# Causal attention of a fused transformer block: reordered casts, sums and transposes, and w(w+2) computed on GpSimd in two instructions

## The reference

```python
tq = jnp.sqrt(1.0 / curv + jnp.sum(q * q, axis=-1, keepdims=True))
tk = jnp.sqrt(1.0 / curv + jnp.sum(k * k, axis=-1, keepdims=True))
inner = jnp.einsum('bhtd,bhsd->bhts', q, k) - tq * jnp.swapaxes(tk, -1, -2)
arg = jnp.maximum(-curv * inner, 1.0 + 1e-07)
dis = jnp.sqrt(1.0 / curv) * jnp.arccosh(arg)
scores = 1.0 / (eps + dis) + _causal_bias(q.shape[-2], k.shape[-2], q.dtype)
return jnp.einsum('bhts,bhsd->bhtd', jax.nn.softmax(scores, axis=-1), v)
```

## Time and profile before

| | |
|---|---|
| three runs | 4958.24, 4977.92, 4982.76 us, median 4977.92 |
| profiled execution | 4974.08 us, of it the span 4972.4 us |
| busy, share of the span | PE 78%, PEld 50%, DVE 69%, ACT 42%, POOL 12% |
| mean granted TensorE clock | 0.88 of full speed |

### The profile page before, as it was taken

How to read it: one execution, slowest core, us unless ns; L and a number is a source line. 1 busy time by engine, 2 the same in 40 slices (tenths; PEclk the granted TensorE clock), 3 DMA queues, 4 the chain that set the end, 5 groups by cost and what they waited for, 6 DMA issues and landing times. The chain is left out here.

```text
span 4972.4 us, 89619 instructions
## 1 busy us (share of the span) xinstructions
PE 3898.1 (78%) x25263; PEld 2472.9 (50%) x25263; DVE 3431.8 (69%) x7462; ACT 2095.3 (42%) x3970; POOL 581.7 (12%) x1014
## 2 busy tenths in 40 slices
PE   6999799800048988857777776888799999799998
PEld 5777588600025555535555554666444444455554
DVE  4555444388967887867777775667677777477777
ACT  1222144476533333336767675233366666011110
POOL 0111100000000000010000000222111111122221
PEclk8999999955569989968888887899799999899999
DMA  2222144488954444444444443777555544211110
GB/s 80 75 73 77 56 172 175 171 242 276 400 213 128 125 129 122 123 89 91 94 94 92 94 93 71 177 194 195 133 123 123 123 121 100 75 51 51 57 54 29
DMA packets 508033, 616.80 MB, mean 124 GB/s; under 512 B 62202, under 2 KB 428509, under 8 KB 507933
## 3 DMA queue, kind: packets, MB, share of 16 engines
q1 hardware_dynamic: 498684, 614.41, 44.3%
q0 software_dynamic: 9248, 1.18, 0.2%
HBM read 345.06 MB, written 269.21 MB: 124 GB/s over the span
## 5 line engine op out<-in xcount | busy, mean ns | idle before, releaser
L1231 PE MATMUL ps<-k_downT,f_o 128*91 128x256 f32 x1152 | 261.2, 386 | 455.2 <-DVE f_o L1139 455.1
L3158 PE MATMUL ps<-m_we,m_xT 128*128 128x512 f32 x1104 | 507.4, 604 | 0.0
L2489 DVE TENSOR_REDUCE e_neg<-ps 128x2 f32<-128x546 f32 x512 | 369.7, 723 | 121.2 <-PE ps L2264 112.1
L1231 PEld LDWEIGHTS ps<-k_downT,f_o 128*91 128x91 f32 x1152 | 183.6, 162 | 524.4 <-issue 456.2
L2426 ACT ACTIVATE e_probT<-ps 128x546 f32<-128x546 f32 x512 | 320.6, 627 | 231.4 <-PE ps L2270 226.8
L3093 DVE SCALAR_TENSOR_TENSOR m_acc<-ps,m_weight,m_acc 128x256 f32<-128x256 f32 x552 | 257.6, 480 | 119.2 <-PE ps L3158 105.4
L3158 PEld LDWEIGHTS ps<-m_we,m_xT 128*128 128x128 f32 x1104 | 203.5, 192 | 212.7 <-issue 195.6
L587 DVE TENSOR_REDUCE b_new<-b_gu 128x1 f32<-128x1638 f32 x64 | 119.0, 1859 | 211.5 <-ACT b_gu L654 211.5
L2264 PE MATMUL ps<-e_k,e_q 96*128 96x273 bf16 x1024 | 213.1, 292 | 28.3 <-POOL e_block_mask L2222 16.1
L654 ACT COPY b_gu<-ps 128x273 f32<-128x273 f32 x384 | 148.5, 387 | 189.0 <-PE ps L692 189.0
L2270 PE MATMUL ps<-e_q,e_k 99*128 99x273 bf16 x1024 | 208.3, 285 | 9.3 <-DMA e_q<-e_shift 1.4
(11 more groups left out here) (375 smaller groups left out, 9040.7 us busy)
## 6 DMA issues: line engine op xcount, KB each, us to landing
s_gate<-b_gu SPq DMA_DIRECT2D x32, 819.0 KB, 4.0
s_up<-b_gu SPq DMA_DIRECT2D x32, 819.0 KB, 3.7
c_g<-s_gate SPq DMA_DIRECT2D x32, 819.0 KB, 7.0
s_gated<-c_g SPq DMA_DIRECT2D x32, 819.0 KB, 8.4
d_g<-s_gated SPq DMA_DIRECT2D x32, 819.0 KB, 10.7
d_u<-s_up SPq DMA_DIRECT2D x32, 819.0 KB, 10.6
s_o<-d_o SPq DMA_DIRECT2D x32, 819.0 KB
f_o<-s_o SPq DMA_DIRECT2D x32, 819.0 KB, 4.6
```

Source lines behind the costliest of these rows:

```text
L1231: last = nc.tensor.matmul(ps[0:R, t // 2, (t % 2) * D:(t % 2 + 1) * D], o[:, u, k, t * R:(t + 1) * R], downT[:, k, :], start=(k == 0), sto ...
L2489: nc.vector.tensor_reduce(neg[:, u, g // 2, :, 4 * (g % 2) + a], ps[:, bank:bank + 2, 0:T], AX.X, ALU.max, negate=True).then_inc(S["looked ...
L3158: last = nc.tensor.matmul(ps[0:R, EBANK[m % 4], :], xT[:, u, k, t * R:(t + 1) * R], we[:, k, 2 * p:2 * p + 2, :].rearrange("p e d -> p (e ...
```

## The change

The product w(w+2) leaves DVE. GpSimd computes it in two instructions, hu = w + 2 and hu = hu * w, with a semaphore `hu2` between them; it waits for the clamp and for the earlier batch's `add_root`, which reads `hu`. Further, PE emits MAIN 3 and PRE 6 to 8 ahead of `turn` 1; ACT does exponential 3 ahead of `first_part_hyp` and exponential 4 ahead of `second_part_hyp`, and `second_part` ahead of two of the `log_of_distance`; DVE does `top_scores` ahead of `remainder_hyp`, `largest` 0 ahead of `third_part_hyp`, and `add_shift` 3 ahead of `third_part`.

```diff
@@ block.gpsimd
-            S["spread"].give(pool)
+            for x in ("spread", "hu", "hu2"):
+                S[x].give(pool)
...
+            def square(n, u):
+                pool.wait_ge(S["wc"].sem, S["wc"].at(n))
+                pool.sem_inc(passed, 1)
+                pool.wait_ge(S["z"].sem, S["z"].at((n[0], n[1] - 1)))
+                pool.sem_inc(passed, 1)
+                nc.gpsimd.tensor_scalar(hu[:], hw[:, u], 2.0, None, ALU.add).then_inc(S["hu2"].sem, 1)
+                pool.wait_ge(S["hu2"].sem, S["hu2"].at(n))
+                nc.gpsimd.tensor_tensor(hu[:], hu[:], hw[:, u], ALU.mult).then_inc(S["hu"].sem, 1)
...
                 if here[MAIN]:
                     spread_hyp(now, u)
+                if here[PRE]:
+                    square(then, tu)
@@ block.tensor
+                emit((MAIN, 3), (PRE, 6), (PRE, 7), (PRE, 8))
                 if mains:
                     turn(now, u, 1, posts)
-                emit((MAIN, 3), (PRE, 6), (PRE, 7), (PRE, 8))
@@ block.scalar
+                    exponential(now, u, b, 3)
                     first_part_hyp(now, u)
-                    exponential(now, u, b, 3)
+                    exponential(now, u, b, 4)
                     second_part_hyp(now, u)
-                    exponential(now, u, b, 4)
                     exponential(now, u, b, 5)
...
                     log_of_distance(then, tu, 2)
+                    second_part(then, tu)
                     log_of_distance(then, tu, 3)
-                    log_of_distance(then, tu, 4)
                 if mains:
                     exponential_hyp(now, u, 2)
                 if pres:
-                    second_part(then, tu)
+                    log_of_distance(then, tu, 4)
@@ block.vector
-            def square(n, u):
-                dve.wait_ge(S["wc"].sem, S["wc"].at(n))
-                nc.vector.scalar_tensor_tensor(out=hu[:], in0=hw[:, u], scalar=2.0, in1=hw[:, u],
-                                               op0=ALU.add, op1=ALU.mult).then_inc(S["hu"].sem, 1)
...
+                if pres:
+                    top_scores(then, tu, b)
                 if mains:
                     remainder_hyp(now, u)
                 if pres:
-                    top_scores(then, tu, b)
                     clamp(then, tu)
+                    largest(then, tu, b, 0)
                 if mains:
                     third_part_hyp(now, u)
                 if posts:
                     divide(post, pu, pi, 3)
                 if pres:
-                    largest(then, tu, b, 0)
-                    square(then, tu)
                     for h in range(1, 4):
                         largest(then, tu, b, h)
...
                 if mains:
                     add_shift(now, u, b, 2)
+                if mains:
+                    add_shift(now, u, b, 3)
                 if pres:
                     third_part(then, tu)
-                if mains:
-                    add_shift(now, u, b, 3)
```

More of the change, by code:

```diff
@@ L1361, in attention_causal @@
         laid = [sem(f"laid{u}") for u in range(2)]
-        S = signals(ctx, nc, "g", look=LOOKS, looked=LOOKS, s=16, exp=17, shifted=NHYP, topm=1, topw=2, wc=1, hu=1,
+        S = signals(ctx, nc, "g", look=LOOKS, looked=LOOKS, s=16, exp=17, shifted=NHYP, topm=1, topw=2, wc=1, hu=1, hu2=1,
                     hl=1, root=1, z=1, l1=1, l2=5, score=1, hneg=3, negm=1, spread=3, turn=2, hi=2, rest=2, mid=2, lo=2,
@@ L1893, in _ @@
         def _(dve):
-            for x in ("looked", "shifted", "topm", "topw", "wc", "hu", "z", "hneg", "negm", "rest", "lo", "rec", "out"):
+            for x in ("looked", "shifted", "topm", "topw", "wc", "z", "hneg", "negm", "rest", "lo", "rec", "out"):
                 S[x].give(dve)
```

## The result

The changed kernel takes 5079.8 us (median of four runs, 5076.7 to 5086.9) against 4977.8 before: ratio 1.0206, 95% interval 1.0184 to 1.0228. It is slower by 102 us, where 13 us were forecast, and outside the stated range. The profiled execution has a span of 5079.9 us, 107.5 more than the one before; all of it lies in the causal stage.

A forecast was written before the change was run, and what follows sets the result against it. A circle of waits across engines, no engine full, bounds the kernel; -2.19 (reordering) and +2.51 (square on POOL) give +0.32 a step, +9.9 over 31 steps, +3.5 for the first square: 4991 us, range 4945 to 5045.

The forecast's parts named there:

- the circle: Causal attention: a closed chain of waits across engines, logarithm to clamp to square to logarithm, sets the 27.30 us step.
- both waits: ACT's 0.80 us before exp_hyp 3 and DVE's 1.39 us for PRE 6; removing them saves 2.19 us a step.
- the price of pass 1: GpSimd's one-input tensor_scalar (w + 2) over 1698 elements: taken as 1.77 us, bounds 1.50 to 3.77.
- the step over 28.1 us: Sign of being wrong: a causal step longer than 28.1 us, where 27.6 us was expected.
- pass 1 above 2.1: Sign of being wrong: GpSimd's w + 2 instruction over 2.1 us, where about 1.8 was expected.
- the stretched third_part_hyp: Sign of being wrong: this DVE instruction, 0.44 us before, stretched to over 1 us.
- the low clock under turn_back 0: Sign of being wrong: PE's granted clock at 0.50 while turn_back 0 runs.
- Pass 2: GpSimd's two-input tensor_tensor, the product hu * w: 3.76 us at 2.10 ns an element.
- The clock: Rival: PE's low clock begins with turn_back 0, costing 0.8 us a step toward distance: +25, 5016 us; 12%.
- pass 1 costs like two inputs: Rival: GpSimd's w + 2 takes 3.77 us instead of 1.77: +64, 5055 us; 13%.
- third_part_hyp excludes POOL: Rival: this DVE instruction and GpSimd's large ones shut each other out, +0.44 us a step: +14, 5005 us; 8%.
- The faster rival: GpSimd multiplies at the one-input rate, product 1.69 us, step 1.8 us shorter: 4927 us; 15%.

The follow-up runs named there:

- the reordering alone: The changed kernel with the square back on DVE behind divide 3, the rest of the change kept: 4951.4 us, ratio to before 0.9946.
- The copy: The changed kernel with GpSimd's first instruction a plain tensor_copy of w into hu, leaving out the addition of 2: 4979.5 us (one execution).
- the pieces: The changed kernel with GpSimd's tensor_scalar sum cut into two instructions of 420 and 1278 elements, same work: 5080.5 us (one execution).
- the matmuls: The reordering alone plus 44 matmuls that only add work, put on TensorE just ahead of turn_back 0: 4930.2 us, ratio to before 0.9899.
- GpSimd alone: The kernel before in its old order, only the square moved to GpSimd in two passes: 5183.0 us, ratio 1.0408.

## Why the prediction was wrong

**The reading of the circle held.** logarithm, ACT, exp_hyp 3, scores, PRE 6, clamp, square: both waits that the reordering was to remove are gone, and distance to clamp fell by 2.3 us where 2.19 were forecast. That the size agrees is in part luck: it does so only in steps whose stretch behind turn_back 2 runs at the full clock, for which the prediction gave no reason, and in most steps of the reordering alone it doesn't.

**The step that failed is the price of pass 1.** "tensor_scalar of 4 elements 0.283 us; one-input affine_select ... 0.88 ns an element", taken as 1.77 with an upper bound of 3.77, measured 4.50. The kind was chosen by the number of inputs. The copy (1.60) shows that a one-input GpSimd instruction can run at that rate; the pieces show that tensor_scalar with a sum doesn't, at 2.55 ns an element. Even the upper end, the two-input price, was too low, and the 5055 us that go with it already lay outside the range. The wrong price is 2.73 of the 3.0 us a step by which the forecast missed (+0.32 forecast, +3.33 measured). Of the signs of being wrong that the prediction names, the step over 28.1 us, pass 1 above 2.1, the stretched third_part_hyp and the low clock under turn_back 0 all came. Why the sum by tensor_scalar costs so much isn't shown, nor what its other operations cost. The Trainium skill, "GPSIMD Engine Reference", section 3.1, gives a small body 1.03 cycles an element, at 1.2 GHz 0.86 ns (an estimate from that page): the copy comes near with 0.94 ns, while tensor_scalar took three times as much.

**Pass 2** was right for the even batches, which use the first half of `hw` (3.76), and too dear for the odd ones (3.19): -0.28 a step in the mean.

**The clock was weighed and put at nothing**, with the rival at 0.8 us a step. It came true in part: 6.97 - 6.34 = 0.63 us a step. The argument that a wait of 3.26 us did no harm, so that a longer one need not, was of no use: in the changed kernel turn_back 0 starts at the low clock behind waits of 7 to 8.5 us, but in most steps of the reordering alone it does so behind 3.2 to 3.4 us. What decides it isn't shown. That this stretch costs about 0.6 to 0.7 us is shown by the matmuls that fill it in the reordering alone (6.97 to 6.24).

**The sum as measured:** +4.99 (clamp to logarithm) + 0.63 - 2.29 = +3.33 us a late step. Between the first and the last logarithm the 31 steps take 99.6 us more, the first one is 8.4 us later (its clamp to logarithm grew by 6.35 us, for which +3.5 was forecast); together 108 of the 107.5 us.

**Of the rivals**, "pass 1 costs like two inputs" had the right place and sign, at too small a price. "third_part_hyp excludes POOL" is right as to DVE (3.38 us instead of 0.44) and wrong as to the cost: the passes were no longer beside it than without. The Trainium skill, "SBUF — State Buffer", "Who interferes with whom", states that a DVE instruction with two inputs in SBUF contends with a GpSimd one that reads SBUF; the trace agrees: 3.38 us beside pass 1. The faster rival, a two-input pass at the one-input rate, is refuted by 3.19 to 3.76.

**What I would also have got wrong:** the reordering alone was worth 24 us and not 2.19 x 31 = 68, since the low clock sits in the stretch from distance to clamp in most of its steps. In the changed kernel that stretch is clear of it in nearly all steps, which accounts for 2.3 of the 3.4 us a step that the reordering was worth there. The rest is that GpSimd alone has 18.7 in the third column where before has 17.5; why wasn't traced. Nor is it settled why a step falls into the one kind or the other; only that behind turn_back 2 the granted clock is 0.53 to 0.66 over 3.6 us in the long kind and 1.00 in the short one.

## What to carry to other kernels

Price an instruction by a row of its own kind on its own engine: on GpSimd the one-input sum was dearer than the two-input one. On a circle of waits, moving work to an idle engine costs its full duration there (8.45 us from clamp to logarithm here, where DVE needed 3.46, or 1.99 without delay); the better answer here was the reordering with the square left on DVE and put first in the queue. And a shorter circle may be paid back by TensorE's low clock, so look at the granted clock stretch by stretch before adding up savings.

## What the runs showed that was not expected

GpSimd, 1698 f32 elements: copy 1.60 us, tensor_scalar with a sum 4.50, tensor_tensor 3.19 or 3.76 by where an operand begins (3.02 in nearly all steps with the same tile as both inputs). In the runs with the copy and with the two-input pass 1, where third_part_hyp reached into pass 2, pass 2 took 0.08 us more (3.27 and 3.84), but not in the first batch, which has no third_part_hyp beside it. Rows of 1698 elements put the second half of hw 6792 bytes on, 8 past a multiple of 64; rows of 1712 remove the difference. Which starts are the quick ones wasn't tried.
